# Expert choice by comparing ranks on VectorE, the down product in two parts, attention rows asked a step ahead

## The chip, the cores and the metric

The kernel runs on one core of a Trainium2 chip. The metric is device time in microseconds (us) of one execution. Every figure of a trace below is from one profiled execution of the kernel before the change.

## What is computed

One transformer layer on x of 4 x 1024 x 128 in float32:

```
h   = x + attention(layernorm(x))          # 16 heads of 8 values, causal softmax, biases bq bk bv bo
z   = layernorm(h)
l   = z @ gate_w.T                          # 8 experts
rw  = sigmoid(max(l)); sel = argmax(l)      # the first of equal logits
out = h + sum over e of (u_e * silu(g_e)) @ w_down[e].T
      with zs = z * rw * (sel == e), g_e = zs @ w_gate[e].T, u_e = zs @ w_up[e].T
```

Each token passes one expert (inner width 64) of eight. The kernel computes all eight for every token and lets only the chosen one through.

## The kernel before, in words

**Two stages.** Attention is done in 16 units (four heads of one of the four batches each). Behind it comes the expert stage: eight steps of 512 tokens, step n being tokens of batch (n-1)//2, half (n-1)%2. The expert stage is what the change touches. Its first product starts at 434.48 us of the span, its last sum ends at 557.8 us.

**One step.** `project3` (L1076) multiplies the attention rows `attn` by `w_o`; VectorE adds the residual, takes mean and variance (`residual`, L873), GpSimd takes the reciprocal root (`rsqrt3`, L595), VectorE normalises (`normalise`, L756) to `xn`. TensorE turns `xn` (`turn_xn`), ScalarE copies it, TensorE makes the `logits`. `route` (L882) on VectorE finds the largest logit, marks the equal ones, multiplies by `ramp` (8 for expert 0 down to 1 for expert 7), takes the largest of these and marks every expert that is not it as refused. ScalarE takes the tanh for the sigmoid, VectorE multiplies the rows by the weight (`xs`, L897), TensorE turns them (`turn_xs`).

**Gate, up, down.** Experts go in four pairs of 64 + 64 rows. For each pair `back` on TensorE (L1105) issues a gate product (`w_g`, 128x512 float32), a bf16 product of `shut` (8 x 512, -1e30 where a column belongs to the expert) with `refused_t`, which adds -1e30 to the gate of every refused expert in the same bank so that its silu is zero, and an up product (`w_u`). ScalarE's `back` (L721) takes the silu, VectorE's `back` (L900) multiplies it by the up product into `hidden`. `down` (L1118) is 16 products of 128x128 in float32 (four token tiles by four pairs, accumulated); `finish` (L906) adds the residual, and SyncE stores the 512 rows.

**Order.** Each engine works off its own list, written out by hand: inside step n stand, between the four pairs, the pieces of the front of step n+1 (`turn_xn`, `logits`, `turn_refused`, `turn_xs`) and `project3` of step n+2. A float32 product is issued as two instructions, a bf16 one as one.

**Loads.** `weigh` (L591) on GpSimd multiplies the summed values `numer` by the inverse sums `denom`, both loaded by SyncE (`load_attn`, L403). SyncE's `reload` (L437) asks for the rows of step n+2 once `attn` of step n is made, and then waits for the output of step n before it stores it; so the next request stands behind that wait. The inverse sums of the last batch are made on VectorE at the start of step 3 (L918).

**At the start of the program** GpSimd builds constants, among them `shut` (L499 to L503), while VectorE splits the first queries and keys into bf16 parts (`take_parts`, L783).

Of the kernel before, what the change touches and what calls it, by code (L numbers as in the profile page):

```python
# [130 lines left out]
def layer_kernel(nc, x, wq_t, wk_t, wv_t, wo_t, bq, bk, bv, bo, gate_t, wg_t, wu_t, wd_t, out):  # L131
# [7 lines left out]
    with ctx:  # L139
        def sb(name, shape, dt=FP32):  # L140
            return ctx.enter_context(nc.sbuf_tensor(name, shape, dt))

        def sem(name):
            return ctx.enter_context(nc.semaphore(name))
# [51 lines left out]
        hit = sb("hit", [P, 2, TPH, EXPERTS])  # L196
        first = sb("first", [P, 2, TPH])
        refused = sb("refused", [P, 2, TPH, EXPERTS], BF16)
        refused_t = sb("refused_t", [EXPERTS, HALF], BF16)
        weight = sb("weight", [P, 2, TPH])  # L200
# [70 lines left out]
        tanh_set = sem("tanh_set")  # L271
        refused_set = sem("refused_set")
        refused_turned = sem("refused_turned")
        refused_t_set = sem("refused_t_set")
        xs_set = sem("xs_set")
# [3 lines left out]
        up_mm = sem("up_mm")  # L279
        silu_set = sem("silu_set")  # L280
        hidden_set = sem("hidden_set")
        down_mm = sem("down_mm")
# [33 lines left out]
        def _(sp):  # L316
# [131 lines left out]
            for b in range(1, BATCH - 1):  # L448
                reload(b)
            for h in range(2):  # L450
                store(BATCH - 1, h)
            for h in range(2):
# [3 lines left out]
        def _(pool):  # L456
# [43 lines left out]
            chain.link(g.affine_select(out=shut[:], in_=shut[:], pattern=[[1, EXPERTS * INNER]], base=0,  # L500
                                       channel_multiplier=-INNER, compare_op=ALU.is_ge, fill=0.0))
            g.affine_select(out=shut[:], in_=shut[:], pattern=[[-1, EXPERTS * INNER]], base=INNER - 1,
                            channel_multiplier=INNER, compare_op=ALU.is_ge, fill=0.0).then_inc(const_set, 1)  # L503
            rsqrt1(4, 2)
# [110 lines left out]
        def _(act):  # L615
# [86 lines left out]

            def copy_refused(n):
                act.wait_ge(refused_turned, n)
                a.activation(refused_t[:], ps[0:EXPERTS, BANK_ROUTE, :].bitcast(BF16)[:, HALF:],
                             ACT.Copy).then_inc(refused_t_set, 1)

# [17 lines left out]

            copy_refused(1)
            copy_xs(1, 0)
            for n in range(1, STEPS + 1):
                n4, h = 4 * (n - 1), (n - 1) % 2
                more = n < STEPS  # L730
                back(n4, 0)
                if more:
                    copy_xn3(n + 1, 1 - h)
                back(n4, 1)
                if more:
                    tanh(n + 1, 1 - h)
                back(n4, 2)
                back(n4, 3)
                if more:
                    copy_refused(n + 1)  # L740
                    copy_xs(n + 1, 1 - h)

        @block.vector
        def _(dve):
# [110 lines left out]
            def invert(b0, b1):  # L855
                v.reciprocal(inv[:, b0:b1], inv[:, b0:b1]).then_inc(inv_set, 1)
# [4 lines left out]
            for u in range(UNITS):  # L861
# [4 lines left out]
                for e in ORDERS[u]:  # L866
                    if e[0] in ("piece", "turn"):
                        take(e)

            def x1_of(b, h):  # L870
                return x_sb[:, b * (2 * TPH) + h * TPH:b * (2 * TPH) + (h + 1) * TPH, :]
# [10 lines left out]
            def route(n, h):  # L882
# [15 lines left out]
                last.then_inc(xs_set, 1)  # L898

            def back(n4, pr):  # L900
                dve.wait_ge(up_mm, n4 + pr + 1)
                dve.wait_ge(silu_set, n4 + pr + 1)
                v.tensor_tensor(hidden[:, pr, :], ps[:, BANK_UP[pr % 2], :], silu[:, pr % 2, :],  # L903
                                ALU.mult).then_inc(hidden_set, 1)
# [6 lines left out]

            residual(1, 0, 0)
            route(1, 0)
            residual(2, 0, 1)
            for n in range(1, STEPS + 1):
                b, h = divmod(n - 1, 2)
                n4 = 4 * (n - 1)
                if n == 3:  # L918
                    dve.wait_ge(sums_in, 16 * BATCH)
                    invert(BATCH - 1, BATCH)  # L920
                back(n4, 0)
                back(n4, 1)
                if n < STEPS:
                    route(n + 1, 1 - h)
                back(n4, 2)
                back(n4, 3)
                if n + 2 <= STEPS:
                    residual(n + 2, b + 1, h)
                finish(n, b, h)

        @block.tensor
        def _(pe):
# [160 lines left out]

            def turn_refused(n, h):
                pe.wait_ge(refused_set, n)
                turned_rows = ps[0:EXPERTS, BANK_ROUTE, :].bitcast(BF16)[:, HALF:]
# [7 lines left out]

            def back(n, n4, h, pr):  # L1105
                if pr == 0:
                    pe.wait_ge(xs_t_set, n)
                    pe.wait_ge(refused_t_set, n)
                cols = slice(pr * P, (pr + 1) * P)
# [5 lines left out]
                mm(ps[:, BANK_UP[pr % 2], :], w_u[:, cols], xs_t[:, h, :], start=True, stop=True  # L1115
                   ).then_inc(up_mm, 1)

            def down(n, n4):  # L1118
                pe.wait_ge(hidden_set, n4 + PAIRS)
                hold(pe, y_set, n - 1)  # L1120
                for i in range(TPH):
                    for pr in range(PAIRS):
                        last = mm(ps[:, BANK_DOWN, i * P:(i + 1) * P], hidden[:, pr, i * P:(i + 1) * P],  # L1123
                                  w_d[:, pr, :], start=(pr == 0), stop=(pr == PAIRS - 1))
                last.then_inc(down_mm, 1)

# [12 lines left out]
            for u in range(UNITS):  # L1139
                for e in ORDERS[u]:  # L1140
# [6 lines left out]
                    else:  # L1147
                        use(e)
            turn_refused(1, 0)
            turn_xs(1, 0)  # L1150
            pe.wait_ge(exp_done, load_at(UNITS, 0))
            pe.wait_ge(sum_set, 2 * UNITS)
            for n in range(1, STEPS + 1):
                n4, h = 4 * (n - 1), (n - 1) % 2
                more = n < STEPS
                back(n, n4, h, 0)
                if more:
                    turn_xn(n + 1, 1 - h)
                back(n, n4, h, 1)
                if more:  # L1160
                    logits(n + 1, 1 - h)
                back(n, n4, h, 2)
                back(n, n4, h, 3)
                if n + 2 <= STEPS:
                    project3(n + 2, h)
                if more:
                    turn_refused(n + 1, 1 - h)
                    turn_xs(n + 1, 1 - h)
                down(n, n4)

# [31 lines left out]
```

## Time and profile before

| | |
|---|---|
| median of 3 runs | 563.52 us (563.22 to 566.83) |
| the profiled execution | 562.29 us, its span 560.6 us |
| TensorE busy | 533.4 us, 95% of the span |
| VectorE busy | 449.8 us, 80% |
| ScalarE busy | 385.0 us, 69% |
| GpSimd busy | 211.2 us, 38% |
| mean granted TensorE clock | 0.984 |

Engines in the profile: PE is TensorE's matmuls, PEld its weight loads, DVE VectorE, ACT ScalarE, POOL GpSimd, SP SyncE. L1112 is line 1112 of the kernel. Records of matmuls are pipelined and their ends modelled: from one start to the next is the safer measure, and the chain of waits gives the part of each piece that lies on the path.

### The profile page before, as it was taken

To read this page: it belongs to the slowest core of one execution; us is meant where nothing else is said; L and a number is where in the kernel's file an instruction comes from. 1 tells how busy PE (TensorE), PEld (TensorE's weight loads), DVE (VectorE), ACT (ScalarE), POOL (GpSimd) and SP (SyncE) were. 2 spreads that over 40 slices of the span, in tenths; PEclk is the share of its full clock that TensorE was granted. 3 is DMA by queue.
4 is the path that set the end of the run, shared out by engine and by line. 5 is a ranking of instruction groups with operands and counts; after the bars stand their busy time and mean duration, and the time that the engine had idled before them with its cause. 6 is when DMAs were issued, how large, how long until landed. Compare 5 with 4: busy or idle time off the path is not lost.

```text
span 560.6 us, 12273 instructions
## 1 busy us (share of the span) xinstructions
PE 533.4 (95%) x4674; PEld 234.5 (42%) x4674; DVE 449.8 (80%) x668; ACT 385.0 (69%) x771; POOL 211.2 (38%) x393
## 2 busy tenths in 40 slices
PE   8559899999999999999999999999988999999996
PEld 6324434333343333433434334334223555666553
DVE  6938899999999999999999999999924655655631
ACT  7224688898998998988989899899886322222221
POOL 5577264443363444533544346314142111111100
PEclk9769999999999999999999999999999999999999
DMA  6151122320211511102232021120030112121000
GB/s 174 30 168 52 37 64 73 111 66 10 65 37 36 168 28 57 56 18 69 80 104 68 10 66 42 43 69 10 7 100 4 48 56 62 56 58 57 19 20 19
DMA packets 27866, 32.45 MB, mean 58 GB/s; under 512 B 4384, under 2 KB 21280, under 8 KB 27808
## 3 DMA queue, kind: packets, MB, share of 16 engines
q1 hardware_dynamic: 27664, 31.28, 19.2%
q8 instruction: 37, 0.61, 0.4%
q10 hardware_dynamic: 144, 0.39, 0.2%
q14 instruction: 21, 0.17, 0.1%
HBM read 20.26 MB, written 11.01 MB: 56 GB/s over the span
## 4 chain that ended last, share of the span: by engine, by line
PE 70%; DVE 18%; ACT 4%; POOL 3%; issue 2%; DMA 2%; ACTq 1%; POOLq 0%; DVEq 0%
PE ps L1062 19%; PE ps L1046 13%; PE ps L1003 8%; DVE top_p L825 7%; DVE top_p L827 6%; PE ps L1115 6%; PE ps L1123 5%; PE ps L1112 5%; ACT prob L681 4%; DVE top_p L820 3%; PE ps L1013 3%; PE ps L947 2%; PE ps L938 2%; PE ps L1113 2%; PE ps L1021 1%
## 5 line engine op out<-in xcount | busy, mean ns | idle before, releaser
L681 ACT ACTIVATE prob<-ps 128x512 f32<-128x512 f32 (+2 forms) x640 | 307.5, 560 | 41.6 <-PE ps L1046 36.8
L827 DVE TENSOR_REDUCE top_p<-ps 128x2 f32<-128x1024 f32 x192 | 223.6, 1217 | 5.4 <-PE ps L1013 1.8
L1046 PE MATMUL ps<-q_rows,k_rows 51*128 51x512 bf16 (+3 forms) x768 | 168.9, 328 | 2.7 <-ACT prob L681 1.4
L1062 PE MATMUL ps<-prob,v_all 128*9 128x512 f32 (+3 forms) x1536 | 156.8, 488 | 0.7 <-ACT sum_sb L672 0.4
L581 POOL TENSOR_SCALAR_AFFINE_SELECT prob<-prob 128x512 f32<-128x512 f32 x128 | 81.4, 636 | 184.8 <-ACT prob L681 183.0
L1003 PE MATMUL ps<-k_rows,q_rows 48*128 48x512 bf16 (+2 forms) x896 | 130.7, 305 | 8.9 <-DMA k_rows<-split_parts 6.9
L1046 PEld LDWEIGHTS ps<-q_rows,k_rows 51*128 51x128 bf16 x768 | 52.4, 93 | 135.4 <-ACT prob L681 120.0
L825 DVE TENSOR_REDUCE top_p<-ps 128x4 f32<-128x1024 f32 x64 | 76.4, 1214 | 3.5 <-PE ps L1013 3.3
L1003 PEld LDWEIGHTS ps<-k_rows,q_rows 48*128 48x128 bf16 x896 | 42.8, 94 | 45.3 <-issue 15.5
L724 ACT ACTIVATE prob<-ps 128x512 f32<-128x512 f32 x32 | 19.1, 597 | 56.0 <-PE ps L1113 56.0
L903 DVE TENSOR_TENSOR prob<-ps,prob 128x512 f32<-128x512 f32 x32 | 22.1, 690 | 36.9 <-PE ps L1115 36.9
L1013 PE MATMUL ps<-shade,pick 64*128 64x128 bf16 (+3 forms) x512 | 51.0, 245 | 0.0
L820 DVE TENSOR_REDUCE top_p<-ps 128x8 f32<-128x1024 f32 x32 | 39.2, 1225 | 14.5 <-PE ps L1013 14.0
L1062 PEld LDWEIGHTS ps<-prob,v_all 128*9 128x9 f32 x1536 | 24.4, 88 | 45.9 <-issue 33.6
L1115 PE MATMUL ps<-xs_t,w_u 128*128 128x512 f32 x64 | 36.0, 645 | 0.0
L1013 PEld LDWEIGHTS ps<-shade,pick 64*128 64x128 bf16 x512 | 31.7, 96 | 7.4
L1112 PE MATMUL ps<-xs_t,w_g 128*128 128x512 f32 x64 | 33.4, 603 | 1.1 <-ACT xs_t L710 1.1
L1123 PE MATMUL ps<-w_d,prob 128*128 128x128 f32 x256 | 30.1, 276 | 0.8 <-DVE prob L903 0.8
L1123 PEld LDWEIGHTS ps<-w_d,prob 128*128 128x128 f32 x256 | 29.2, 192 | 1.7 <-DVE prob L903 1.6
L593 POOL TENSOR_TENSOR rest<-qk 128x512 f32<-128x512 f32 x8 | 10.1, 1268 | 46.5 <-DMA qk<-inverse_sums 46.5
L636 ACT ACTIVATE qk<-ps,b_qk 128x512 f32<-128x512 f32 x16 | 11.0, 688 | 18.1 <-PE ps L947 18.1
L947 PE MATMUL ps<-xn_t,w_qkv 128*128 128x512 f32 x32 | 20.1, 745 | 0.8 <-ACT xn_t L630 0.8
(90 smaller groups left out, 430.1 us busy)
## 6 DMA issues: line engine op xcount, KB each, us to landing
split_parts<-part SPq DMA_DIRECT2D x6, 768.0 KB, 5.1
q_rows<-split_parts SPq DMA_DIRECT2D x31, 96.0 KB
k_rows<-split_parts SPq DMA_DIRECT2D x31, 96.0 KB
value_sums<-sum_sb SPq DMA_DIRECT2D x128, 18.0 KB
x_sb<-x SPq DMA_DIRECT2D x8, 256.0 KB, 4.5
qk<-value_sums SPq DMA_DIRECT2D x8, 256.0 KB, 3.6
qk<-inverse_sums SPq DMA_DIRECT2D x8, 256.0 KB, 3.8
out<-y SPq DMA_DIRECT2D x8, 256.0 KB, 2.3
```

The source lines that it names most:

```text
L581: g.affine_select(out=blockv, in_=blockv, pattern=[[0, GH], [1, P]], base=0, channel_multiplier=-1, compare_op=ALU.is_ge, fill=0.0).then_i ...
L681: a.activation(prob[:, i % NB, g0:g0 + heads, 0:cols], ps[:, load_at(u, n) % 3, 0:heads * cols].rearrange("p (s t) -> p s t", s=heads), AC ...
L820: return v.tensor_reduce(top_p[:, place, qts, :].rearrange("p x (r s) -> p r x s", r=2), banks.rearrange("p r (x s t) -> p r x s t", x=2, ...
L825: return v.tensor_reduce(top_p[:, place, qt, :], banks.rearrange("p r (s t) -> p (r s) t", s=2), AX.X, ALU.max)
L827: return v.tensor_reduce(top_p[:, place, qt, s:s + 3:2], banks, AX.X, ALU.max)
L1003: last = mm(ps[:, first_bank + rg, m * width:(m + 1) * width], q_rows[rows, k, s, qt * P:(qt + 1) * P], k_rows[rows, k, s, k0:k0 + width], ...
L1013: last = mm(dst, pick[rows, e, :], shade[rows, e, None, 64 * e:P].to_broadcast((64, len(blocks), P - 64 * e)), start=False, stop=True, ski ...
L1046: last = mm(ps[:, l % 3, m * cols:(m + 1) * cols], k_rows[rows, k, s + m, j * P:(j + 1) * P], q_rows[rows, k, s + m, c * HALF + q0:(c + 1) ...
L1062: last = mm(ps[32 * g:32 * g + HD + 1, BANK_V, q0:HALF], v_all[:, b, j, first_head + g, :], prob[:, i % NB, g, 0:n], start=(j == 0), stop= ...
L1112: mm(gate, w_g[:, cols], xs_t[:, h, :], start=True, stop=False)
L1115: mm(ps[:, BANK_UP[pr % 2], :], w_u[:, cols], xs_t[:, h, :], start=True, stop=True).then_inc(up_mm, 1)
L1123: last = mm(ps[:, BANK_DOWN, i * P:(i + 1) * P], hidden[:, pr, i * P:(i + 1) * P], w_d[:, pr, :], start=(pr == 0), stop=(pr == PAIRS - 1))
```

## The change

What it does, part by part:

- **Choice.** `shut`, `refused`, `refused_t` and their products go. `route` ends with the largest of the ramp, a `rank` per token. TensorE's `spread_rank` multiplies it, repeated over 128 columns, with the bf16 identity, so that each of 128 partitions holds the ranks of the 512 tokens; ScalarE copies them to `rank_b`. VectorE's new `choose` compares `rank_b` with the rank of each partition's expert (`rank_of`) and multiplies the silu by the answer, in place, one 128x512 instruction for each pair. The up product is then multiplied as before.
- **Order.** TensorE issues gate and up apart, the gate products ahead; `down` goes in two parts, pairs 0 and 1 before `spread_rank` and `turn_xs`, pairs 2 and 3 behind. On VectorE `route` stands between the first two `back`, the weighing of rows (`weigh_rows`) behind the second.
- **Loads.** SyncE asks for the rows of step n behind the output of step n-4 instead of n-3; the inverse sums of the last batch are made at the start of step 2.

```diff
-        shut = sb("shut", [EXPERTS, EXPERTS * INNER], BF16)
+        rank_of = sb("rank_of", [P, PAIRS])
...
+        BANK_RANK, FIRST_RANK = BANK_GATE[0], BANK_UP[1]
...
-            def reload(b):
-                for h in range(2):
-                    sp.wait_ge(attn_set, b * 2 + h + 1)
-                    load_attn(b + 1, h)
-                    store(b, h)
+            def reload(n):
+                b, h = divmod(n - 1, 2)
+                sp.wait_ge(attn_set, n - 2)
+                load_attn(b, h)
...
-            reload(0)
+            reload(3)
+            reload(4)
+            store(0, 0)
             sp.wait_ge(inv_set, 2)
             store_inverse(BATCH - 1)
-            sp.wait_ge(inv_out, 16 * BATCH)
-            for b in range(1, BATCH - 1):
-                reload(b)
+            for n in range(5, STEPS + 1):
+                if n == STEPS - 1:
+                    sp.wait_ge(inv_out, 16 * BATCH)
+                reload(n)
+                store(*divmod(n - 4, 2))
...
-            last.then_inc(const_set, 1)
-            chain.link(g.memset(shut[:], MASKED))
-            chain.link(g.affine_select(out=shut[:], in_=shut[:], pattern=[[1, EXPERTS * INNER]], base=0,
...
-            g.affine_select(out=shut[:], in_=shut[:], pattern=[[-1, EXPERTS * INNER]], base=INNER - 1,
...
+            last.then_inc(const_set, 2)
...
-            def copy_refused(n):
...
+            def copy_rank(n, h):
+                act.wait_ge(rank_mm, n)
+                hold(act, hidden_set, 4 * (n - 2))
+                a.activation(rank_b[:, h, :], ps[:, BANK_RANK if n > 1 else FIRST_RANK, :], ACT.Copy).then_inc(rank_b_set, 1)
...
-                chain.link(v.tensor_reduce(first[:, h, :], hit[:, h], AX.X, ALU.max))
-                v.tensor_tensor(refused[:, h], hit[:, h],
-                                first[:, h, :, None].to_broadcast((P, TPH, EXPERTS)),
-                                ALU.not_equal).then_inc(refused_set, 1)
+                v.tensor_reduce(rank[:, h, :], hit[:, h], AX.X, ALU.max).then_inc(rank_set, 1)
...
+            def choose(n, h, pr):
+                n_pr = 4 * (n - 1) + pr + 1
+                dve.wait_ge(rank_b_set, n)
+                dve.wait_ge(silu_set, n_pr)
+                v.scalar_tensor_tensor(silu[:, pr % 2, :], rank_b[:, h, :], rank_of[:, pr:pr + 1],
+                                       silu[:, pr % 2, :], ALU.is_equal, ALU.mult).then_inc(chosen_set, 1)
...
-            def turn_refused(n, h):
...
+            def spread_rank(n, h):
+                pe.wait_ge(rank_set, n)
+                bank = BANK_RANK if n > 1 else FIRST_RANK
+                hold(pe, silu_set, 4 * (n - 1) - 1)
                 for i in range(TPH):
-                    last = nc.tensor.transpose(turned_rows[:, i * P:(i + 1) * P], refused[:, h, i, :], ident_b[:])
-                last.then_inc(refused_turned, 1)
+                    last = mm(ps[:, bank, i * P:(i + 1) * P], rank[:, h, i:i + 1].to_broadcast((P, P)),
+                              ident_b[:], start=True, stop=True)
+                last.then_inc(rank_mm, 1)
...
-                gate = ps[:, BANK_GATE[pr % 2], :]
-                mm(gate, w_g[:, cols], xs_t[:, h, :], start=True, stop=False)
-                mm(gate, shut[:, cols], refused_t[:], start=False, stop=True).then_inc(gate_mm, 1)
+                mm(ps[:, BANK_GATE[pr % 2], :], w_g[:, pr * P:(pr + 1) * P], xs_t[:, h, :], start=True, stop=True
+                   ).then_inc(gate_mm, 1)
...
+            def down(n, n4, prs):
+                if prs[0] == 0:
+                    hold(pe, y_set, n - 1)
+                pe.wait_ge(hidden_set, n4 + prs[-1] + 1)
+                for pr in prs:
+                    for i in range(TPH):
```

TensorE, one step of the expert stage (n = 3 or later). In the kernel before; `ident,xn` is `turn_xn`, `ident,xs` is `turn_xs`:

```order
1298 L1112 MATMUL ps<-xs_t,w_g 128x512
1299 L1113 MATMUL ps<-refused_t,shut 128x512
1300 L1115 MATMUL ps<-xs_t,w_u 128x512
1301 L938 MATMUL ps<-ident,xn 128x128 x4
1302 L1112 MATMUL ps<-xs_t,w_g 128x512
1303 L1113 MATMUL ps<-refused_t,shut 128x512
1304 L1115 MATMUL ps<-xs_t,w_u 128x512
1305 L1090 MATMUL ps<-w_gate,xn_t 128x8 x4
```

The same place in the changed kernel, through to the end of the step:

```order
1247 L1134 MATMUL ps<-xs_t,w_g 128x512 x2
1248 L959 MATMUL ps<-ident,xn 128x128 x4
1249 L1139 MATMUL ps<-xs_t,w_u 128x512
1250 L1134 MATMUL ps<-xs_t,w_g 128x512
1251 L1111 MATMUL ps<-w_gate,xn_t 128x8 x4
1252 L1139 MATMUL ps<-xs_t,w_u 128x512
1253 L1134 MATMUL ps<-xs_t,w_g 128x512
1254 L1139 MATMUL ps<-xs_t,w_u 128x512 x2
1255 L1100 MATMUL ps<-w_o,rest 128x128 x4
1256 L1148 MATMUL ps<-w_d,prob 128x128 x8
1257 L1121 MATMUL ps<-ident_b,rank 128x128 x4
1258 L959 MATMUL ps<-ident,xs 128x128 x4
```

The bf16 product between gate and up is gone, two gate products stand ahead of the turn, and half of the down product (L1148) stands ahead of the ranks.

VectorE, one step of the changed kernel (`prob<-ps,prob` at L916 is `back`, `hidden` and `silu` lying in the buffer `prob`):

```order
319 L910 SCALAR_TENSOR_TENSOR prob<-rank_b,rank_of,prob 128x512 x2
320 L916 TENSOR_TENSOR prob<-ps,prob 128x512
321 L891 TENSOR_REDUCE best<-ps 128x4
322 L893 TENSOR_TENSOR hit<-ps,best 128x32
323 L895 TENSOR_TENSOR hit<-hit,ramp 128x32
324 L896 TENSOR_REDUCE rank<-hit 128x4
325 L916 TENSOR_TENSOR prob<-ps,prob 128x512
326 L900 TENSOR_SCALAR weight<-weight 128x4
327 L902 TENSOR_SCALAR xs<-xn,weight 128x128 x4
328 L910 SCALAR_TENSOR_TENSOR prob<-rank_b,rank_of,prob 128x512 x2
329 L916 TENSOR_TENSOR prob<-ps,prob 128x512 x2
330 L882 TENSOR_TENSOR x_sb<-ps,x_sb 128x512
```

Four instructions of 128x512 (L910) have come in, one small one of `route` has gone; the residual of a later step (L882) still stands behind all of them.

## Rows read from the trace of the kernel before

**Rows 1.** Busy time in one stretch of the expert stage; us (count) for PE, PEld, DVE, ACT, POOL; then clock.
```profile
500.00:512.00 12.00, 12.00 (x65) 7.37 (x64) 7.12 (x23) 3.78 (x7) 2.46 (x3) 1.00 0.16 45
```
**Rows 2.** Chain of waits, one step: start us, us on the path, what.
```profile
481.73 0.86 PE ps L1112 x2
482.59 0.32 PE ps L1113
482.91 1.05 PE ps L1115 x2
483.96 0.44 PE ps L938 x4
...
486.63 0.79 PE ps L1090 x8
487.43 0.96 PE ps L1112 x2
...
491.99 0.89 PE ps L1079 x8
492.88 0.32 PE ps L1098 x4
493.20 0.59 PE ps L938 x4
493.79 3.57 PE ps L1123 x32
497.36 0.86 PE ps L1112 x2
```
**Rows 3.** Chain of waits, first product of the stage, and the last step.
```profile
434.48 1.10 PE ps L1112 x2
...
543.49 0.86 PE ps L1112 x2
...
553.21 3.85 PE ps L1123 x32
...
557.08 0.69 DVE y L909
```
**Rows 4.** Timeline of VectorE in one step: start, us, line, idle before in brackets.
```profile
472.99 0.87 DVE L897 TENSOR_SCALAR xs<-xn,weight 128x128 f32<-128x128 f32 x4
...
476.36 0.69 DVE L903 TENSOR_TENSOR prob<-ps,prob 128x512 f32<-128x512 f32 x1 [1.54 <-PE ps L1115]
477.36 0.69 DVE L876 TENSOR_TENSOR x_sb<-ps,x_sb 128x512 f32<-128x512 f32 x1 [0.32 <-PE ps L1079]
...
480.85 1.11 DVE L758 TENSOR_SCALAR xn<-x_sb,moments,rstd 128x128 f32<-128x128 f32 x4 [1.48 <-POOL rstd L466]
481.88 0.68 DVE L909 TENSOR_TENSOR y<-ps,x_sb 128x512 f32<-128x512 f32 x1
```
**Rows 5.** Timeline of GpSimd: weighing of attention rows, idle before it in brackets.
```profile
487.43 1.26 POOL L593 TENSOR_TENSOR rest<-qk 128x512 f32<-128x512 f32 x1 [6.62 <-DMA qk<-inverse_sums]
```
**Rows 6.** VectorE's small product L889 over the run: ns min/median/max.
```profile
L889 DVE TENSOR_TENSOR hit<-hit,ramp x8: 191/782/1307, 429.8 to 534.8; 128x32 f32<-128x32 f32 x8
```
**Rows 7.** Timeline of ScalarE: copy of the turned refusals.
```profile
477.61 0.59 ACT L705 ACTIVATE refused_t<-ps 8x512 bf16<-8x512 bf16 x1 [1.71 <-PE ps L1098]
```
**Rows 8.** Three lines of VectorE at the start: ns min/median/max, first and last start.
```profile
L785 DVE CAST part<-qk x2: 696/882/1068, 12.3 to 19.1; 128x1024 bf16<-128x1024 f32 x2
L786 DVE TENSOR_TENSOR rest<-qk,part x2: 1224/1364/1504, 13.0 to 20.2; 128x1024 f32<-128x1024 f32 x2
L788 DVE CAST part<-rest x2: 694/838/983, 14.3 to 21.7; 128x1024 bf16<-128x1024 f32 x2
```
**Rows 9.** Timeline of GpSimd at the start: the last of three steps on `shut`.
```profile
20.68 1.48 POOL L502 TENSOR_SCALAR_AFFINE_SELECT shut<-shut 8x512 bf16<-8x512 bf16 x1
```
**Rows 10.** Chain of waits at the start, where VectorE's split ends.
```profile
22.75 1.24 DVE part L793
24.00 2.31 DMA split_parts<-part
```

More of the change, by code:

```diff
@@ L196, in layer_kernel @@
         hit = sb("hit", [P, 2, TPH, EXPERTS])
-        first = sb("first", [P, 2, TPH])
-        refused = sb("refused", [P, 2, TPH, EXPERTS], BF16)
-        refused_t = sb("refused_t", [EXPERTS, HALF], BF16)
+        rank = sb("rank", [P, 2, TPH], BF16)
+        rank_b = sb("rank_b", [P, 2, HALF])
         weight = sb("weight", [P, 2, TPH])
@@ L271, in layer_kernel @@
         tanh_set = sem("tanh_set")
-        refused_set = sem("refused_set")
-        refused_turned = sem("refused_turned")
-        refused_t_set = sem("refused_t_set")
+        rank_of_set = sem("rank_of_set")
+        rank_set = sem("rank_set")
+        rank_mm = sem("rank_mm")
+        rank_b_set = sem("rank_b_set")
         xs_set = sem("xs_set")
@@ L731, in _ @@
                 back(n4, 0)
+                back(n4, 1)
                 if more:
                     copy_xn3(n + 1, 1 - h)
-                back(n4, 1)
+                back(n4, 2)
                 if more:
                     tanh(n + 1, 1 - h)
-                back(n4, 2)
                 back(n4, 3)
                 if more:
-                    copy_refused(n + 1)
+                    copy_rank(n + 1, 1 - h)
                     copy_xs(n + 1, 1 - h)
@@ L868, in _ @@
                         take(e)
+            for e in range(EXPERTS):
+                last = v.memset(rank_of[INNER * (e % 2):INNER * (e % 2 + 1), e // 2:e // 2 + 1], float(EXPERTS - e))
+            last.then_inc(rank_of_set, 1)
             def x1_of(b, h):
@@ L917, in _ @@
                 n4 = 4 * (n - 1)
-                if n == 3:
+                if n == 2:
                     dve.wait_ge(sums_in, 16 * BATCH)
                     invert(BATCH - 1, BATCH)
+                choose(n, h, 0)
+                choose(n, h, 1)
                 back(n4, 0)
+                if n < STEPS:
+                    route(n + 1, 1 - h)
                 back(n4, 1)
                 if n < STEPS:
-                    route(n + 1, 1 - h)
+                    weigh_rows(n + 1, 1 - h)
+                choose(n, h, 2)
+                choose(n, h, 3)
                 back(n4, 2)
@@ L1103, in turn_xs, with gate, up @@
                 turn_tiles(xs[:, h], BANK_TURN).then_inc(xs_turned, 1)
-            def back(n, n4, h, pr):
+            def gate(n, n4, h, pr):
                 if pr == 0:
+                    pe.wait_ge(rank_b_set, n)
                     pe.wait_ge(xs_t_set, n)
-                    pe.wait_ge(refused_t_set, n)
-                cols = slice(pr * P, (pr + 1) * P)
                 hold(pe, silu_set, n4 + pr - 1)
-                gate = ps[:, BANK_GATE[pr % 2], :]
-                mm(gate, w_g[:, cols], xs_t[:, h, :], start=True, stop=False)
-                mm(gate, shut[:, cols], refused_t[:], start=False, stop=True).then_inc(gate_mm, 1)
+                mm(ps[:, BANK_GATE[pr % 2], :], w_g[:, pr * P:(pr + 1) * P], xs_t[:, h, :], start=True, stop=True
+                   ).then_inc(gate_mm, 1)
+            def up(n4, h, pr):
                 hold(pe, hidden_set, n4 + pr - 1)
-                mm(ps[:, BANK_UP[pr % 2], :], w_u[:, cols], xs_t[:, h, :], start=True, stop=True
+                mm(ps[:, BANK_UP[pr % 2], :], w_u[:, pr * P:(pr + 1) * P], xs_t[:, h, :], start=True, stop=True
                    ).then_inc(up_mm, 1)
[L1118 to L1122, printed above, removed]
+            def down(n, n4, prs):
[4 more added lines that the diff above has]
+                    for i in range(TPH):
                         last = mm(ps[:, BANK_DOWN, i * P:(i + 1) * P], hidden[:, pr, i * P:(i + 1) * P],
-                                  w_d[:, pr, :], start=(pr == 0), stop=(pr == PAIRS - 1))
-                last.then_inc(down_mm, 1)
+                                  w_d[:, pr, :], start=(pr == 0 and i == 0), stop=(pr == PAIRS - 1),
+                                  skip_group_check=True)
+                if prs[-1] == PAIRS - 1:
+                    last.then_inc(down_mm, 1)
             def lead_in(i):
@@ L1148, in _ @@
                         use(e)
-            turn_refused(1, 0)
+            spread_rank(1, 0)
             turn_xs(1, 0)
             pe.wait_ge(exp_done, load_at(UNITS, 0))
-            pe.wait_ge(sum_set, 2 * UNITS)
             for n in range(1, STEPS + 1):
@@ L1155, in _ @@
                 more = n < STEPS
-                back(n, n4, h, 0)
+                gate(n, n4, h, 0)
+                gate(n, n4, h, 1)
                 if more:
                     turn_xn(n + 1, 1 - h)
-                back(n, n4, h, 1)
+                up(n4, h, 0)
+                gate(n, n4, h, 2)
                 if more:
                     logits(n + 1, 1 - h)
-                back(n, n4, h, 2)
-                back(n, n4, h, 3)
+                up(n4, h, 1)
+                gate(n, n4, h, 3)
+                up(n4, h, 2)
+                up(n4, h, 3)
                 if n + 2 <= STEPS:
                     project3(n + 2, h)
+                if n == 1:
+                    pe.wait_ge(sum_set, 2 * UNITS)
+                down(n, n4, (0, 1))
                 if more:
-                    turn_refused(n + 1, 1 - h)
+                    spread_rank(n + 1, 1 - h)
                     turn_xs(n + 1, 1 - h)
-                down(n, n4)
+                down(n, n4, (2, 3))
 def kernel(L0_attn_x, L0_attn_Wq, L0_attn_bq, L0_attn_Wk, L0_attn_bk, L0_attn_Wv, L0_attn_bv, L0_attn_Wo,
```

19 lines of the change are left out of this document (8 added, 11 removed).

## The prediction

> **What bounds the kernel now.** I looked first at the busy times of each engine in the expert stage, the only stage the change rebuilds. In 12 us from 500 us TensorE is busy all 12.00, at full clock (1.00, 2.4 GHz), VectorE 7.12 and ScalarE 3.78 [rows 1]. So the second view is the chain of waits: it shows TensorE pieces only, from one step to the next. A step lasts from 481.73 to 497.36, 15.63 us, and its pieces add up to it with no wait between them [rows 2]. Only in the last step do VectorE and the end of the down product come into the chain [rows 3]. What is taken off TensorE's list in this stage therefore comes off the time, until another engine's list is longer than TensorE's new one. That second limit is what the views of VectorE [rows 4] and GpSimd [rows 5] are for.
>
> **What TensorE gets rid of.** Four bf16 products with `shut` in each step, 0.32 us each on the path: 1.28 us. There is more. A float32 product of 128x512 takes 0.86 us on the path behind another float32 product (gate behind the turn or behind the down product), but the up product, which stands behind the short bf16 one, takes 1.05 [rows 2]: 0.20 more, four times. In the new order every up stands behind a float32 product, so I take 0.86 for it and count 4 x 0.20 = 0.80. The product behind the logits keeps its 0.96 (gate before, up now). Both together: 2.08 us of each step.
>
> The Trainium skill, "TensorE: Matmul & The Clock Gate", section "Back-to-back issue gap", gives 216 ns for a product of 512 columns and has the next weights loaded ahead of running products; by that a step would lose 4 x 0.22 = 0.9 us, some 7 us over eight steps, and the up product would have nothing to give back. The row (0.32, and 1.05 beside 0.86) disagrees, and the sum goes by the row.
>
> **What TensorE keeps or gets.** `spread_rank` is four bf16 products of 128 columns, as the turning of `refused` was (0.32 for four [rows 2]); that its weights are 128 columns wide instead of 8 may add at most 0.1, which I leave in the range. The turn behind it stays at 0.59. The down product is the same 16 products in two parts, each with its own weights as before: 3.57 us, nothing gained. New step of TensorE: 15.63 - 2.08 = 13.55 us.
>
> **VectorE, a new limit.** It gets four `choose` of 128x512 in float32 from two inputs in SBUF. No row shows one. The nearest are 0.69 us (128x512, one input in PSUM [rows 4]) and 1.22 for 1024 elements from SBUF [rows 8], that is about 0.6 for 512. I take 0.69; bounds 0.60 and, for an instruction that goes twice over its elements, 1.38. The same price comes from the Trainium skill, "VectorE: DVE Perf Modes", section on the errata: (N+151)/0.96 ns gives 0.69 for 512.
>
> Then there is the port that VectorE shares with GpSimd. VectorE's little product L889 takes 0.19 us, but up to 1.31 where it meets `weigh` [rows 6], which takes 1.26 [rows 5]: it waits for nearly all of it. Before, `weigh` waits 6.62 us for its data [rows 5] and starts in the middle of a step. Now its data are asked a step earlier and lie ready, so it starts straight behind the reciprocal root of the step before, at the very moment at which VectorE's `normalise` (same form as `xs`) wants to start. GpSimd goes on without a semaphore and should be first: 1.17 us on VectorE, in each step that has a `weigh` behind its root (steps 1 to 5).
>
> So I lay VectorE's list from the second `back` of one step to the turn of `xn` in the next, start to start. After that `back` (0.62): weight and four `xs` 0.99, two `choose` 1.38, two `back` 1.24, residual to `normalise` 3.49 (477.36 to 480.85, with the wait for the root), the port 1.17, `normalise` with its signal 1.13 [rows 4]: 10.0 us. TensorE then turns, and issues up, gate, logits, up, with its signal: 0.44 + 0.86 + 0.86 + 0.79 + 0.96 + 0.2 = 4.1 [rows 2]. The loop closes in 14.1 us, 0.5 more than TensorE's own 13.55. TensorE will wait these 0.5 us at `turn_xn`, a wait that has taken the place of part of the saving. The rest of VectorE's work (two `choose`, one `back`, route, `y`) lies under the 4.1 us of TensorE and the gaps; ScalarE's copy of the ranks costs what the copy of the refusals did (0.59 [rows 7]) and is done about 1 us before the next gate.
>
> **The sum over the stage.** Step 1: 15.8 (434.48 to 450.3) becomes 14.2, with half a us of wait for the second `xn`, which VectorE finishes too late for the earlier turn: -1.6. Steps 2, 4, 5, 6: 15.63 becomes 14.1: 4 x -1.5 = -6.0. Step 3 pays some of VectorE's reciprocal, moved to step 2: -1.3. Step 7 has no `project3` and no port wait ahead of it: 14.9 becomes 12.7: -2.2. The last step, 543.49 to the end of `y` at 557.77 [rows 3], is 14.3 us; now 8 x 0.86 for gate and up, two half down products of 1.8, signal and `y` 0.9: 11.4, as the first half starts without waiting for the last `hidden`: -2.9 (three quarters of a us of it the wait ahead of 553.21 [rows 3]). Total -14.0.
>
> **Asking for rows earlier** is worth nothing by itself: no TensorE wait for them shows. It costs the 1.17 above. If the cover were gone, nothing would be late: rows asked behind output n-4 have two steps.
>
> **The start.** GpSimd's three steps on `shut` are gone. VectorE's second round of L785, L786, L788 took 1.07, 1.50 and 0.98 where the first took 0.70, 1.22 and 0.69 [rows 8], while GpSimd worked on `shut` [rows 9]; the chain runs through them to the DMA that everything waits for [rows 10]. I take the 0.9 us as gained; the bounds are 0 and 0.94. Eight tiny memsets on VectorE before the stage lie in its idle time.
>
> **The numbers.** -14.0 - 0.9 = -14.9 us. The profiled execution of 562.29 becomes 547.4; the median, 563.52, lies 1.2 above that execution, and becomes 548.6. I forecast 548.5.
>
> **Rivals.**
> 1. *The up product does not get faster*: its 0.20 belong to something other than the bf16 product ahead of it. Speaking for it: no row shows a gate directly followed by an up. Against: three other kinds of neighbour give 0.86. Then only 1.28 come off each step, the loop of 14.1 lies under TensorE's 14.35, and the total is about 8 x 1.28 + 1 + 0.9, 551.5. Chance 0.12.
> 2. *The port does not block*, as VectorE gets it first or `weigh` comes at another moment. The Trainium skill, "SBUF — State Buffer", section "SBUF: two separate sides", has it that whoever starts first holds the pair for the whole instruction; no row shows both ready at once. Then the waits of 0.5 go and the time is 546. Chance 0.2.
> 3. *VectorE becomes the bound*: `choose` at 0.9 to 1.2 us. Two of them lie in the loop, and two more delay it. At 0.9 the steps are 14.55, total 551; at 1.2 they are 15.4 and the total is 557. Chance 0.12.
> 4. *Slower than before*: `choose` goes twice over its elements. At 1.38 us VectorE's own list for a step (four of them, 5.5, beside 9.5 of other work with the root's wait, and 1.2 of port) is about 16 us, longer than the old 15.63; the short last steps and the start just pay for it, about 563. That is the point from which it decides. At 1.6 us each step is past 17 and the time is 569. For it: two inputs and a scalar per partition in one instruction is a form that no row shows. Against: every row of VectorE with two inputs runs near one element a clock. Chance 0.04 at or beyond the point, 0.03 of them over 1% slower.
> 5. *The change buys nothing*, as the time of the products is taken up elsewhere, within 1%: 0.03.
>
> The forecast's own case (546.5 to 550.5) has 0.49. The range holds it with rivals 1 and 2 and the cheaper half of 3: 545 to 555, a little over 0.8 with what I don't know of the clock and the start. A measurement of this kernel tells about 1% (5.6 us) from no change; faster than 557.9 is 0.91, within 1% 0.06, slower 0.03.
>
> **What the profile after would show.** No line with `shut`; each up at 0.86 on the chain; steps of 14.1 from gate to gate, with one wait of TensorE for VectorE's `normalise` of about 0.5 in each; `normalise` taking about 2.3 instead of 1.11 in steps 1 to 5, with `weigh` beside it; `choose` at 0.69; no wait before the last down product; VectorE's L785 at the start at 0.70 both times. The prediction is wrong if `choose` is far from 0.69, if up stays at 1.05, or if TensorE waits at a gate for the copied ranks.

## The result, and the profile after

The changed kernel takes 550.54 us in the median of 4 runs (547.36 to 550.8), the kernel before 565.17 beside it (4 runs, 563.22 to 567.9): a ratio of 0.9725, 95% interval 0.9664 to 0.9786. Timed once more (experiment 10), the ratio was 0.9690 (0.9648 to 0.9733). The forecast was 548.5 in a range of 545 to 555, and 14.9 us less than before; the medians say 14.6 less.

| profiled execution | before | after |
|---|---|---|
| time; span | 562.29; 560.6 us | 550.8; 549.1 us |
| first score product of attention | 34.27 | 33.61 |
| first gate product | 434.48 | 438.83 |
| end of the last `y` | 557.77 | 546.29 |
| expert stage (the two lines above) | 123.29 | 107.46 us |
| mean granted clock | 0.984 | 0.972 |

The stage got 15.8 us shorter, more than the span (11.5), because it began 4.35 us later, although the first score product came 0.66 us earlier. Chain of waits of the changed kernel, one step (start us, us on the path, what), which answers to [rows 2]:

```profile
481.01 0.04 DVE xn L760
481.05 1.17 issue
482.22 0.42 DVE xn L760 x2
...
482.73 0.35 DVE xn L760
...
483.12 0.66 PE ps L959 x4
483.78 0.86 PE ps L1139 x2
484.64 0.86 PE ps L1134 x2
485.50 0.79 PE ps L1111 x8
486.29 0.96 PE ps L1139 x2
487.25 0.86 PE ps L1134 x2
488.11 1.72 PE ps L1139 x4
489.83 0.91 PE ps L1100 x8
...
490.81 0.68 DVE prob L916
491.49 0.61 DVE x_sb L882
...
492.12 0.88 DVE stats L752 x4
```

Up (L1139) costs 0.86 like gate (L1134), and the chain now leaves TensorE: it runs over VectorE's last `back`, the residual and `normalise` (L760) to the turn of `xn` (L959). From 483.12 to the same turn at 496.99 are 13.87 us. The second row, 1.17 us of "issue", lies between the first and the second of the four instructions of `normalise`, while GpSimd's `weigh` runs; it is read here as the wait at the port that VectorE and GpSimd share, and experiment 3 moves `weigh` away to test that. Timeline of GpSimd, VectorE and TensorE at that place (start, us, line, idle before in brackets), to be read beside [rows 4, 5]:

```profile
480.95 1.27 POOL L595 TENSOR_TENSOR rest<-qk 128x512 f32<-128x512 f32 x1
481.01 2.06 DVE L760 TENSOR_SCALAR xn<-x_sb,moments,rstd 128x128 f32<-128x128 f32 x4 [1.47 <-POOL rstd L473]
...
483.12 0.66 PE L959 MATMUL ps<-ident,xn 128*128 128x128 f32 x4 [0.32 <-DVE xn L760]
```

`weigh` starts 0.06 us ahead of `normalise`, which takes 2.06 us instead of 1.11, and TensorE waits 0.32. The turn behind this wait takes 0.66 on the chain, and 0.44 where TensorE did not wait ([rows 2] has such a turn), so the step pays about 0.5.

**What took 4.35 us ahead of the stage.** Busy time in stretches of 5 us (PE, PEld, DVE, ACT, POOL busy with counts; then PEclk, the granted clock) in the changed kernel:

```profile
410.00:415.00 5.00, 4.95 (x25) 0.68 (x17) 0.00 (x0) 3.17 (x8) 1.27 (x2) 0.51 0.52 146
415.00:420.00 5.00, 4.74 (x29) 0.79 (x28) 0.00 (x0) 4.14 (x8) 2.53 (x2) 0.50 0.38 116
420.00:425.00 5.00, 4.90 (x36) 1.65 (x32) 1.94 (x9) 3.08 (x6) 1.17 (x2) 0.97 0.03 8
...
430.00:435.00 5.00, 5.00 (x34) 3.71 (x30) 2.68 (x10) 1.83 (x5) 0.82 (x2) 0.56 0.00 0
```

TensorE ran this end of attention, which the change does not touch, at 1.2 GHz twice (a granted clock of 0.50 to 0.51 for about 10 us, then a mean of 0.56 over the 5 us from 430). The profiled execution of before had 1.00 from 385 us to the stage. Nothing ties this to the change: the profile of experiment 5, which is the kernel before with a padded constant, has the same two dips (0.53 and 0.50 from 410 us, 0.58 from 430) and its first gate product as late, at 439.83. Over all runs the kernel before has mean clocks from 0.969 (566.9 to 568.3 us) to 0.987 (562.3 to 563), the changed kernel from 0.969 (551.2) to 0.991 (545.95). At an equal 0.978, before takes 563.9 to 565.4 and the changed kernel 547.1 to 547.4: about 17 us apart. Single whole times of this kernel are therefore read together with the clock, and the experiments below by their stage and step.

### The profile page after: what moved, and what is told of

Same layout as the page of the kernel before. It is cut to its first block, busy times and chain, and to the rows that moved or that the text cites. A ratio compares the mean times of both kernels' runs of the same rounds, so it can differ in the third digit from the quotient of the medians.

```text
span 549.1 us, 12283 instructions
## 1 busy us (share of the span) xinstructions
PE 521.0 (95%) x4642; PEld 235.7 (43%) x4642; DVE 468.0 (85%) x700; ACT 384.3 (70%) x771; POOL 207.7 (38%) x390
## 4 chain that ended last, share of the span: by engine, by line
PE 65%; DVE 21%; ACT 4%; POOL 4%; issue 3%; DMA 1%; ACTq 1%; POOLq 0%; DVEq 0%
PE ps L1083 21%; PE ps L1067 14%; PE ps L1024 8%; DVE top_p L827 7%; DVE top_p L829 6%; PE ps L1139 5%; DVE top_p L822 4%; PE ps L1134 3%; ACT prob L683 3%; PE ps L1034 3%; PE ps L968 3%; PE ps L1148 2%; PE ps L959 2%; PE ps L1100 1%; PE ps L1111 1%
## 5 line engine op out<-in xcount | busy, mean ns | idle before, releaser
L1083 PE MATMUL ps<-prob,v_all 128*9 128x512 f32 (+3 forms) x1536 | 160.3, 499 | 0.4 <-ACT sum_sb L674 0.4
L822 DVE TENSOR_REDUCE top_p<-ps 128x8 f32<-128x1024 f32 x32 | 39.2, 1225 | 14.7 <-PE ps L1034 14.2
L1134 PE MATMUL ps<-xs_t,w_g 128*128 128x512 f32 x64 | 31.5, 594 | 0.8 <-ACT xs_t L712 0.8
L1139 PE MATMUL ps<-xs_t,w_u 128*128 128x512 f32 x64 | 32.0, 602 | 0.0
L1148 PE MATMUL ps<-w_d,prob 128*128 128x128 f32 x256 | 31.0, 275 | 0.0
L1148 PEld LDWEIGHTS ps<-w_d,prob 128*128 128x128 f32 x256 | 29.9, 192 | 1.0 <-issue 1.0
L472 POOL TENSOR_SCALAR spread<-moments 128x4 f32<-128x4 f32 x8 | 1.8, 230 | 67.2 <-DVE moments L755 67.2
L910 DVE SCALAR_TENSOR_TENSOR prob<-rank_b,rank_of,prob 128x512 f32<-128x512 f32 x32 | 22.7, 740 | 3.1 <-ACT prob L726 2.9
L708 ACT ACTIVATE rank_b<-ps 128x512 f32<-128x512 f32 x8 | 4.8, 596 | 27.2 <-PE ps L1121 27.2
L760 DVE TENSOR_SCALAR xn<-x_sb,moments,rstd 128x128 f32<-128x128 f32 x32 | 13.6, 487 | 11.8 <-POOL rstd L473 11.8
```

The source lines that it names most:

```text
L822: return v.tensor_reduce(top_p[:, place, qts, :].rearrange("p x (r s) -> p r x s", r=2), banks.rearrange("p r (x s t) -> p r x s t", x=2, ...
L1083: last = mm(ps[32 * g:32 * g + HD + 1, BANK_V, q0:HALF], v_all[:, b, j, first_head + g, :], prob[:, i % NB, g, 0:n], start=(j == 0), stop= ...
L1134: mm(ps[:, BANK_GATE[pr % 2], :], w_g[:, pr * P:(pr + 1) * P], xs_t[:, h, :], start=True, stop=True).then_inc(gate_mm, 1)
L1139: mm(ps[:, BANK_UP[pr % 2], :], w_u[:, pr * P:(pr + 1) * P], xs_t[:, h, :], start=True, stop=True).then_inc(up_mm, 1)
```

## The experiments

All stage times run from the first gate product to the end of the last `y`, in the profiled execution.

### 1. The kernel before without its bf16 product

```diff
-                mm(gate, w_g[:, cols], xs_t[:, h, :], start=True, stop=False)
-                mm(gate, shut[:, cols], refused_t[:], start=False, stop=True).then_inc(gate_mm, 1)
+                mm(gate, w_g[:, cols], xs_t[:, h, :], start=True, stop=True).then_inc(gate_mm, 1)
```

> The kernel before with the 32 bf16 products of shut left out and nothing else (so refused experts come through; all other work stays). Theory A (a bf16 product of 0.32 us also makes the float32 product behind it 0.20 longer): steps of 15.63 become 15.63 - 2.08 = 13.55 us, the up product 0.86 on the chain, the whole run 16 to 17 us shorter. Theory B (only the products' own 0.32 count, up keeps 1.05): steps of 14.35, 10 us shorter. Theory C (0.22 for each, the length of 512 columns): 14.75, 7 us shorter. The clock of TensorE in the last stretch of attention is one thing to watch: its two dips in the changed kernel (about 410 to 420 and 430 to 437 us) should not depend on this edit.

550.9 us, ratio 0.9764 (0.9714 to 0.9814). This kernel leaves the refusal out, so its output is another; all other work is the same. Steps of 13.57 us (492.90 to 506.47), up at 0.86. Theory A holds: 2.06 us of each step came from 1.28 us of products. The stage is 107.8 us and not less, because step 3 took 14.7 us (464.45 to 479.17). Its chain shows why:

```profile
465.45 0.87 DVE inv L856
...
466.34 1.68 DMA inverse_sums<-inv
...
468.03 0.52 SPq L405
...
468.59 3.71 DMA qk<-inverse_sums
...
472.37 1.28 POOL rest L593
```

With shorter steps, the rows of step 5, asked behind the output of step 2 and behind the store of the last inverse sums, come too late: `project3` waits 0.88 us for them. Under steps of 15.63 the same order was hidden.

### 2. The changed kernel, rows asked as before

```diff
-                reload(n)
                 store(*divmod(n - 4, 2))
+                reload(n)
```

> The changed kernel, but the rows of step n asked behind the output of step n-3 again instead of n-4 (the two calls in SyncE's loop change places). Theory A (asking earlier puts weigh beside normalise and costs 0.94 us on VectorE and the wait of TensorE there): normalise back to 1.11, but weigh (1.26) now falls in the middle of the step, beside the row weighing and choose, which read two SBUF inputs or the two-port form and lie in the same loop; so the loop keeps most of its 13.87, between 13.41 and 13.9. Theory B (asking ahead is needed): TensorE waits at project3 for attention rows, steps over 14. Theory C (the port is nothing): 13.87 with the same wait.

550.41 us, ratio 0.974 (0.9698 to 0.9781). Stage 109.1 us, 1.6 more than the changed kernel. Both A and B are seen. From step 3 on `normalise` is back at 1.11 to 1.12, but `weigh` now falls on the two `choose` (2.41 for two instead of 1.40; steps 3 and 5) or on the row weighing (1.94 instead of 0.87; steps 4 and 6). From turn to turn of `xn` these four steps take 14.57, 13.93, 14.63 and 13.88, where the changed kernel has 13.87. In steps 3 and 5 TensorE waits 0.97 at `project3` besides, in step 3 over this chain:

```profile
465.77 0.39 SPq L438
...
466.20 0.52 SPq L409
...
466.77 4.79 DMA qk<-inverse_sums
...
471.62 1.61 POOL rest L595
...
473.28 1.16 PE ps L1100 x8
```

### 3. `weigh` behind `normalise`

```diff
             def weigh(b, h):
                 pool.wait_ge(attn_in[h], b * 32 + 32)
+                if b * 2 + h >= 3:
+                    pool.wait_ge(xn3, b * 2 + h)
```

> The changed kernel, but GpSimd's weigh of step 4 and later waits until normalise of the step before is done (one wait on xn3). It then runs beside y (one input in PSUM, not held up before) and the first choose, ahead of a wait of 0.7 us for the logits. Theory A (the port at normalise is what closes the loop at 13.87 instead of TensorE's own 13.41): normalise back to 1.1, steps of 13.4 in steps 2 to 6, no wait at the turn of xn, 2 to 3 us off the stage of 107.5 us (step 2 keeps part of its 1.27 wait, which is the reciprocal's). Theory B (VectorE's load, not the port): the block moves to choose and the steps stay at 13.8.

544.87 us, ratio 0.9637 (0.9594 to 0.968). The chain of a step is TensorE alone again, from 461.21 to 474.55, 13.34 us:

```profile
461.21 1.72 PE ps L1136 x4
462.93 0.44 PE ps L961 x4
463.37 0.86 PE ps L1141 x2
...
467.70 1.72 PE ps L1141 x4
469.42 0.89 PE ps L1102 x8
470.31 1.79 PE ps L1150 x16
472.09 0.22 PE ps L1123 x4
472.32 0.44 PE ps L961 x4
472.76 1.79 PE ps L1150 x16
474.55 1.72 PE ps L1136 x4
```

Theory A: `weigh` beside `normalise` was what closed the loop. The wait did not vanish from VectorE: two `choose` now take 2.06 us instead of 1.40, but in front of VectorE's wait for the logits (0.45 us are still left of it). Stage 104.4 us, 3.0 less than the changed kernel. One of these 3.0 is step 2 (13.8 instead of 14.8): its wait at the turn fell from 1.27 to 0.27. The expectation put part of that wait down to the reciprocal, but in the changed kernel the reciprocal starts at 455.86, behind that turn (455.39). Two `weigh` lay on the way to it, one on the row weighing of step 1 (1.83 instead of 0.87) and one on `normalise`; this edit moves the second alone.

### 4. Each `choose` twice

```diff
+        spare = sb("spare", [P, PAIRS, HALF])
...
+                v.scalar_tensor_tensor(spare[:, pr, :], rank_b[:, h, :], rank_of[:, pr:pr + 1],
+                                       silu[:, pr % 2, :], ALU.is_equal, ALU.mult)
...
```

> The changed kernel with each choose issued twice (the first into a spare buffer), 32 more VectorE instructions of 128x512. Theory A (the loop over VectorE bounds the step, and two of the four choose lie in it): each step of the loop gets at least 2 x 0.66 = 1.3 us longer, plus what the other two exceed the 0.74 us that VectorE waits for the logits, 0.6: 13.87 becomes 15.2 to 15.8, the whole run about 11 to 16 us longer, close to the kernel before. Theory B (TensorE bounds the step): under 13.9.

561.88 us, ratio 0.9915 (0.9885 to 0.9946). Steps of 15.49 (481.17 to 496.66), stage 119.9 us, 12.5 longer. Theory A. By these steps I estimate that the kernel would be as slow as before if a `choose` cost 1.4 to 1.5 us; as it is, one starts every 0.66 us (recorded 0.74):

```profile
490.62 0.75 DVE L912 SCALAR_TENSOR_TENSOR spare<-rank_b,rank_of,prob 128x512 f32<-128x512 f32 x1
491.29 0.75 DVE L914 SCALAR_TENSOR_TENSOR prob<-rank_b,rank_of,prob 128x512 f32<-128x512 f32 x1
```

### 5. The bf16 product over all 128 rows

```diff
-        shut = sb("shut", [EXPERTS, EXPERTS * INNER], BF16)
+        shut = sb("shut", [P, EXPERTS * INNER], BF16)
...
-        refused_t = sb("refused_t", [EXPERTS, HALF], BF16)
+        refused_t = sb("refused_t", [P, HALF], BF16)
...
+            g.memset(refused_t[:], 0.0)
...
```

> The kernel before with shut and refused_t laid out over all 128 partitions, zeros below the eight experts: the same 32 bf16 products, now 128 rows by 128 columns instead of 8 by 128, the result the same. The changed kernel's spread_rank (128 by 128, bf16) took 0.22 us for four with 0.44 for the turn behind it, where the old turning of the refusals (128 by 8) took 0.32 and 0.59. Theory A (it is the partly filled array, not the data type, whose weight loads are not hidden): the shut product falls from 0.32 to 0.22 and the up product behind it from 1.05 to 0.86; steps of 15.63 become 14.4, the run 10 us shorter. Theory B (change between bf16 and float32): both stay, steps of 15.6.

559.15 us in its one run, stage 114.8 us, steps of 14.44 (484.56 to 499.00). Chain, beside [rows 2]:

```profile
486.94 0.86 PE ps L1113 x2
487.80 0.22 PE ps L1114
488.01 0.86 PE ps L1116 x2
...
494.52 0.32 PE ps L1099 x4
494.84 0.59 PE ps L939 x4
```

Theory A. The same bf16 product with zeros in 120 more rows costs 0.22 instead of 0.32 and leaves up at 0.86. So the extra time belongs to the partly filled array and not to the change of data type, which is the same in both. The turning of the refusals, still 8 columns wide, stays at 0.32 and 0.59 in the same trace. Timelines of weight loads (PEld) and products show where the time went (start, us), first the kernel before, then this run:

```profile
482.52 0.09 PEld L1113 LDWEIGHTS ps<-refused_t,shut 8*128 8x128 bf16 x1 [0.76 <-issue]
482.53 0.38 PE L1113 MATMUL ps<-refused_t,shut 8*128 8x512 bf16 x1
482.84 0.30 PEld L1115 LDWEIGHTS ps<-xs_t,w_u 128*128 128x128 f32 x2 [0.23 <-issue]
482.84 1.12 PE L1115 MATMUL ps<-xs_t,w_u 128*128 128x512 f32 x2
...
484.83 0.10 PEld L1114 LDWEIGHTS ps<-refused_t,shut 128*128 128x128 bf16 x1 [0.24 <-issue]
485.26 0.41 PEld L1116 LDWEIGHTS ps<-xs_t,w_u 128*128 128x128 f32 x2 [0.33 <-issue]
485.48 1.02 PE L1116 MATMUL ps<-xs_t,w_u 128*128 128x512 f32 x2
```

With 8 rows the load takes 0.09 and starts 0.01 before its product, and the load for up starts only with up itself (482.84). With 128 rows the load takes 0.10 but starts at 484.83, while the gate product still runs, and the load for up is 0.22 ahead of its product. The load is not longer with few rows, it is not made ahead. By the Trainium skill, "TensorE: Matmul & The Clock Gate", section "Step-by-step: what each phase is for", the next weights are loaded while the product before still runs; the full array agrees, 8 rows or 8 columns do not.

Padding alone gives back 1.19 us of the 2.06 in each step. The rest, 0.87, is the four products themselves at 0.22. Step 3 is longer here too (15.6), with a wait of 0.93 at `project3` as in experiment 1.

### 6. The constant `shut` built for nobody

```diff
-            last.then_inc(const_set, 2)
+            last.then_inc(const_set, 1)
+            chain.link(g.memset(shut[:], MASKED))
...
```

> The changed kernel with GpSimd's three steps that build shut put back (nobody reads it). Theory A (they held up VectorE's split of the first queries by 0.9 us through the shared port): L785, L786, L788 of the second half take 1.07, 1.50, 0.98 again and the first unit starts 1.3 us later, at the 34.27 of the kernel before instead of 33.61 and with the slower stretch behind it. Theory B (the start moved by chance): the times at the start stay as in the changed kernel. Either way the dips of TensorE's clock at the end of attention may come or not; if they hang on where the start lies, they are gone here.

550.66 us in its one run. VectorE's three lines take 1.07, 1.50 and 0.98 again (0.68, 1.22 and 0.69 in the changed kernel), yet the first score product is at 33.58, as in the changed kernel. The whole start lay 0.78 us earlier here: `normalise` of the first attention rows began at 15.06 instead of 15.84. From there to the first request for the rows of the split it is 10.49 us (15.06 to 25.55), 9.57 in the changed kernel (15.84 to 25.41) and 10.52 before (15.86 to 26.38). So A holds, at 0.95 us. Behind that request the last transfer blurs it: it took 3.89, 4.07 and 3.76 us in these three, and 4.63 in another profile of the changed kernel (experiment 10). Two dips of the clock are in this profile too; with one run that says little on whether they hang on where the start lies.

### 7. The down product in one part

```diff
-                down(n, n4, (0, 1))
...
-                down(n, n4, (2, 3))
+                down(n, n4, (0, 1, 2, 3))
```

> The changed kernel with the down product in one part, behind the turn of xs. Theory A (the split orders the same work otherwise and is worth something only in the last step, where it fills the wait for the last hidden): steps 2 to 6 stay at 13.87, and the last step gets 0.2 to 0.8 longer than its 11.17 (535.12 to the end of y). Theory B (the split gives ScalarE time for the ranks): the gate of the next step has the same wait or less, since ranks and rows come earlier here; then a split that is not needed.

549.11 us in its one run, stage 110.8 us, 3.3 more. Steps in the middle are 13.86 (490.45 to 504.31), so the split is worth nothing there, as theory A has it; the loop only closes at another place, the last `hidden` (0.25 us of wait ahead of the down product). The last step takes 12.5 us (532.00 to 544.52) instead of 11.2, since TensorE waits for VectorE's last products. Step 1 takes 14.9 instead of 13.4 and step 7 13.8 instead of 12.4, with waits of 1.22 and 1.14 at the same place; step 2 is 0.9 shorter. The split is worth more in the last step than expected (0.2 to 0.8), and something in steps 1 and 7, where nothing was expected. Theory B is not borne out.

### 8. Filler products against the falling clock

```diff
...
                         load(u, e[2])
+                        if u == UNITS - 1 and e[2] >= 4:
+                            mm(ps[:, 4 if project_out else BANK_ROUTE, 0:2 * P], ident_b[:],
+                               pick[:].rearrange("p e t -> p (e t)"), start=True, stop=True)
```

> The third experiment's kernel (weigh behind normalise) with one bf16 product of 128x256 (0.11 us, into a bank that nobody reads) behind each of the 36 score products of the last attention unit from the fifth on, where TensorE waits in small pieces for ScalarE. In the changed kernel TensorE's clock fell to half (0.50) for about 10 us from 410 and again for about 6 from 430, in one other run once, in two others not at all; each dip cost 2.3 to 3.4 us. Theory A (the fall follows these small waits, and the filler keeps the clock up): clock 1.00 in every profile from 400 on, the runs spread less, and the median falls by up to 2 us against 544.9. Theory B (the products lie on the path, which is TensorE's two thirds of the time): up to 2 us longer, and the clock as before.

551.3 us, ratio 0.9763 (0.972 to 0.9806), 6 us slower than experiment 3. In the profile the clock is 1.00 from 400 us to the end of the stage, but the first gate starts at 440.81 instead of 433.73. The fillers lie on the path, as theory B has it, and cost three times what it allowed (up to 2 us). Whether they kept the clock up stays open: experiments 3 and 4 had no dip in their profiles without them, and the mean clocks of the six runs here, 0.972 to 0.984, lie as wide as those of experiment 3 (0.975 to 0.984).

### 9 and 10. Experiment 3 and the changed kernel once more, together

> The third experiment's kernel (weigh behind normalise) once more, beside the changed kernel on the same chip. Theory A (its gain is the port at normalise, 5 steps of about half a us, and more in step 2): 2.5 to 4 us under the changed kernel of the next run; stage from the first gate to the end of y 103 to 105 us against 107.5. Theory B (its better time came from TensorE's clock, which did not dip in that profile): no difference beyond 1 us.

> The changed kernel as it is, beside the run before this one. Stage of 107.5 us from the first gate to the end of y, steps of 13.87, whatever the clock does at the end of attention; the runs between 547 and 551, by how often the clock dips (0.972 to 0.984 in the mean).

545.38 us, ratio 0.9662 (0.9625 to 0.9699), and 547.09 us, ratio 0.969 (0.9648 to 0.9733), against 564.74. The intervals overlap. The stages are 104.4 and 107.2 us, as the first time (104.4 and 107.5). The stage says 3 us; the whole times, between dips of the clock worth 1 to 6 us (the first gate product of the changed kernel and its variants, the fillers aside, lies between 433.73 without a dip and 439.44 with two), only lean that way (544.9 and 545.4 against 550.5 and 547.1). Experiment 3 is the best version found.

## Why the prediction was right

**What TensorE gets rid of: right in size, wrong in its reason.** 2.08 us a step were predicted; experiment 1 shows 2.06. I tied the 0.20 us to a bf16 product ahead of a float32 one. Experiment 5 puts them down to the product's 8 rows. `spread_rank` fits that: predicted 0.32 with 0.59 for the turn behind it, measured 0.22 and 0.44, with weights that fill the array. No run widened the old 8 columns alone, so for columns this is a comparison of two different products. TensorE's own step is 13.34 and not 13.55. That rival 1 (1.28 us only) did not come is settled by the up rows at 0.86.

**VectorE as the new limit: right, a little smaller.** The loop was laid out at 14.1 us and measured 13.87. VectorE's side of it took 9.70 (473.42 to 483.12; 10.0 predicted), TensorE's 4.16 (4.1 predicted). `choose` starts every 0.66 us (taken 0.69). The port cost 0.95 us (taken 1.17, where the rows named for it, 1.31 against 0.19, give 1.12): the first of the four instructions of `normalise` took its usual 0.34, only the second was held, and took 1.29. TensorE waits 0.32 in steps 3 to 6 (taken 0.5), but the whole loop is 0.53 above TensorE's own 13.34, as the turn behind a wait costs 0.22 more. Rival 2 (no block) is out by the row of 2.06, and experiment 3 shows what it would have given. Rivals 3 and 4 did not come, but their mechanism can happen: experiment 4 doubles what `choose` takes, to 1.32, and lands at 0.9915, with steps of 15.49, where the two rivals' prices (15.4 at 1.2, about 16 at 1.38) would give some 15.8.

**The sum over the stage.** Predicted -14.0, measured -15.8. Step 1 came out at 13.4 instead of 14.2, because the second `xn` was done in time; step 2 at 14.8 instead of 14.1, with a wait of 1.27 at the turn, as two `weigh` met VectorE on the way to it. Steps 3 to 6 at 13.87 gave about 1.8 each where 1.3 and 1.5 were counted. Step 7 took 12.4 (predicted 12.7), the last 11.2 (11.4).

**Asking for rows earlier: the step that was wrong in its reason.** I wrote that it was worth nothing by itself and cost the port's wait. The first half holds only for steps of 15.63. Experiments 1 and 2 show that with shorter steps the old order makes `project3` wait for its rows (a chain of store, request and landing of some 6 us), and that `weigh` costs VectorE about as much wherever it falls in the loop. With the earlier requests the stage is 1.6 us shorter. What they did cost could be had back by one wait.

**The start.** Predicted -0.9; the three lines of VectorE lost 0.96 us as laid out, the request behind them came 0.95 earlier, counted from `normalise`, and the first score product 0.66, because the transfer in between took 4.07 instead of 3.76. There is no more to gain from VectorE there: TensorE and ScalarE, with the other half's product and copy, are next late (the copy ends at 25.37, where VectorE's half lands at about 25.3).

**The absolute number, and how much of it was luck.** 548.5 was forecast from a median of 563.52, which was 565.17 beside the changed kernel. That is most of the 2.0 us between forecast and result. That the difference came out so close (-14.6 for -14.9) is luck in part. The stage gave 1.8 us more than the sum has, and at an equal clock the two kernels are about 17 us apart; dips of the clock ahead of the stage, which no term of the sum covers, took some 2 us back in the changed kernel's runs.

## What to carry to other kernels

A small product between large ones can cost more than its columns, if it fills only a few rows of the array (shown here for 8 rows; for 8 columns the rows only fit): look at what the next product takes, beside one with another neighbour, and at when its weights are loaded, and try padding with zeros before rebuilding anything. Here that would have given 1.19 us of each step, and the rebuilding 1.76. When steps get shorter, every request that was hidden under the old step has to be placed again, and so has every instruction that shares a port: lay the loop through each engine, not only through the one that was full. Where the clock of the untouched stage moves by as much as the edit, judge by the stage.

## What the runs showed of the hardware that I had not expected

- A bf16 product of 512 columns takes 0.32 us on the path and makes the float32 product behind it 0.20 longer with 8 rows of weights, and takes 0.22 and adds nothing with 128 rows, 120 of them zero (experiment 5). In both cases the load itself takes 0.09 to 0.10; with 8 rows it starts only with its product. Four products of 128 columns take 0.32 with 8 columns of weights (the turning of the refusals) and 0.22 with 128 (`spread_rank`).
- GpSimd's `weigh`, ready at the same time as VectorE's `normalise`, started 0.06 us ahead of it in steps 2 to 6 and held it up for 0.95 of its own 1.27 us. VectorE's first instruction of the four still ran unheld.
- TensorE's granted clock fell from 1.00 to 0.50 for about 10 us in the same untouched stretch in some executions and not in others. What TensorE did just before does not tell the two apart: in the 5 us from 405 us, at a clock of 1.00 in all of them, it was busy 3.85 us (the changed kernel), 4.20 (experiment 10) and 4.24 (experiment 5) where the clock then fell at about 410, and 3.85 (experiment 2), 4.17 (experiment 3) and 4.24 (the kernel before) where it held. The cause stays open.
